# Base product of an expert-mixed FFN kernel by Strassen's algorithm over pairs of tiles

## What is computed

```python
y      = einsum('boi,bih->boh', agg_w, x) + agg_b[:, :, None]     # mixing over channels
base   = einsum('bsd,od->bso', y, base_W)                         # 1024 x 1024, the large product
logits = einsum('bsd,ed->bse', y, router_W)                       # 8 experts
rw     = top-2 of softmax(logits), divided by their sum
mid    = einsum('bsd,edr->bser', y, lora_A) * w_dense[..., None]  # 8 experts x rank 16 = 128 columns
out    = x + base + 2 * einsum('bser,erd->bsd', mid, lora_B)
```

## Time and profile before

| | |
|---|---|
| three runs | 1066.89, 1067.04, 1068.67 us; median 1067.04 |
| profiled execution | 1067.76 us, its span 1065.9 us |
| TensorE busy | 1050.6 us (99%) |
| VectorE busy | 444.5 us (42%) |
| ScalarE busy | 142.2 us (13%) |
| GpSimd busy | 18.9 us (2%) |
| mean granted TensorE clock | 0.995 |
| DMA | 79.64 MB, mean 75 GB/s |

### The profile page before, as it was taken

How to read it: one execution, slowest core, us unless ns; L and a number is a source line. 1 busy time by engine, 2 the same in 40 slices (tenths; PEclk the granted TensorE clock), 3 DMA queues, 4 the chain that set the end, 5 groups by cost and what they waited for, 6 DMA issues and landing times.

```text
span 1065.9 us, 17562 instructions
## 1 busy us (share of the span) xinstructions
PE 1050.6 (99%) x6386; PEld 1047.3 (98%) x6386; DVE 444.5 (42%) x1318; ACT 142.2 (13%) x310; POOL 18.9 (2%) x19
## 2 busy tenths in 40 slices
PE   6899999999999999999999999999999999999998
PEld 5899999999999999999999999999999999999998
DVE  5344344344344344344344344344344344344344
ACT  6311111111111111111111111111111111111110
POOL 4200000000000000000000000000000000000000
PEclk9899999999999999999999999999999999999999
DMA  7312212212212212212212212212212212212211
GB/s 208 112 44 87 83 48 86 78 51 86 82 47 86 75 54 86 74 56 86 72 57 86 73 56 86 71 58 86 67 62 86 66 63 86 68 61 86 69 39 60
DMA packets 48895, 79.64 MB, mean 75 GB/s; under 512 B 22472, under 2 KB 31432, under 8 KB 48848
## 3 DMA queue, kind: packets, MB, share of 16 engines
q1 hardware_dynamic: 39376, 45.87, 15.5%
q10 hardware_dynamic: 9504, 33.56, 8.0%
HBM read 43.76 MB, written 33.59 MB: 73 GB/s over the span
## 4 chain that ended last, share of the span: by engine, by line
PE 97%; DVE 1%; SPq 1%; DMA 0%; ACT 0%; issue 0%; DVEq 0%
PE acc L391 77%; PE y_ps L366 11%; PE acc L415 8%; PE acc L293 1%; PE y_ps L400 1%; DMA x_sb<-in_L_cond_weight 0%; DVE mixk L597 0%; PE y_ps L310 0%; DVE w_lo L572 0%; SPq L201 0%; DVE out_sb L696 0%; ACT mixk L487 0%; PE acc L345 0%; DVE agg L180 0%; SPq L194 0%
## 5 line engine op out<-in xcount | busy, mean ns | idle before, releaser
L391 PE MATMUL acc<-w_hi,y_hi 128*128 128x388 f32 (+1 forms) x1536 | 395.8, 364 | 0.6 <-DVE y_lo L638 0.6
L391 PE MATMUL acc<-w_hi,y_lo 128*128 128x388 f32 (+1 forms) x1536 | 356.7, 339 | 0.0
L391 PE MATMUL acc<-w_lo,y_hi 128*128 128x388 f32 (+1 forms) x1536 | 356.6, 338 | 0.0
L391 PEld LDWEIGHTS acc<-w_lo,y_hi 128*128 128x128 f32 x1536 | 277.7, 188 | 0.0
L391 PEld LDWEIGHTS acc<-w_hi,y_lo 128*128 128x128 f32 x1536 | 276.6, 188 | 0.0
L391 PEld LDWEIGHTS acc<-w_hi,y_hi 128*128 128x128 f32 x1536 | 247.9, 190 | 1.0 <-issue 0.9
L366 PE MATMUL y_ps<-mix_w,x_sb 128*128 128x128 f32 x1024 | 196.5, 275 | 0.0
L366 PEld LDWEIGHTS y_ps<-mix_w,x_sb 128*128 128x128 f32 x1024 | 186.4, 190 | 0.0
L643 DVE COPY logits<-acc 128x8 f32<-128x8 f32 x64 | 10.7, 167 | 296.0 <-PE acc L391 296.0
L630 DVE TENSOR_TENSOR y_sum<-y_ps,bias_sb 128x512 f32<-128x512 f32 x128 | 88.5, 691 | 78.6 <-PE y_ps L366 78.6
L638 DVE TENSOR_TENSOR y_lo<-y_sum,y_hi 128x512 fp32r<-128x512 f32 x128 | 88.0, 687 | 45.5 <-ACT y_hi L521 45.5
(11 more groups left out here) (76 smaller groups left out, 283.7 us busy)
## 6 DMA issues: line engine op xcount, KB each, us to landing
x_sb<-in_x SPq DMA_DIRECT2D x64, 512.0 KB, 4.8
out<-out_sb ACTq DMA_DIRECT2D x63, 512.0 KB, 4.9
w_stage<-in_L_ffn_base_W SPq DMA_DIRECT2D x8, 512.0 KB, 7.4
bias_sb<-bias_rows SPq DMA_DIRECT2D x64, 64.0 KB, 3.6
mix_w<-agg SPq DMA_DIRECT2D x126, 16.0 KB, 4.2
x_sb<-in_L_cond_weight SPq DMA_DIRECT2D x4, 128.0 KB
la_raw<-in_L_ffn_lora_A SPq DMA_DIRECT2D x8, 64.0 KB, 3.1
out_sb<-in_L_ffn_lora_B SPq DMA_DIRECT2D x1, 512.0 KB, 5.5
```

The lines of the kernel that those rows point to most:

```text
L391: last = nc.tensor.matmul(acc[s][g][:, 0:z - a], y[:, s, c * P:(c + 1) * P], w[:, c, a:z], start=(c == 0 and first), stop=(c == NC - 1 and ...
```

## The change

The base product is computed for two tiles at once, as a 2x2 by 2x2 block product in the seven-product form of Strassen's algorithm (Winograd's variant). The blocks are: rows by sample half, contraction by half (512), output by half (512).

- Operands of rows: A11, A12, A22 and the sums S1 to S4. VectorE writes the blocks (`add_bias`, four a pair), GpSimd makes the four sums (`sums`, `more_sums`), ScalarE the seven high parts (`split_high`), VectorE the seven low parts (`split_low`).
- Operands of weights: B11, B21, B22 and T1 to T4, made once in the setup, 28 groups where there were 16, three of the sums by GpSimd (2048 columns each) and T3 by accumulating products with `ident` and `neg_ident`.
- Products: seven of four chunks by three splits. Four of them carry a `lora_A` and router half at their end (`product_with_side`): each is two matmuls of 376 and 272 columns, the latter over two separate stretches of the weights and in a second PSUM bank. Three are single matmuls of 512 columns (`product`).
- The output halves are put together in `out_sb`, into which `x` has been loaded a second time: eight additions by VectorE (`add_into`), three of `u2` by GpSimd (`add_u2`), after one of VectorE that makes `u2`.
- `up` has 512 columns a matmul, four groups of three a pair, in the order P1, up21, up22, P2, P7, P6, P5, P4, up11, P3, up12, where the first two ups are of the pair before. The mixing products of the next pair stand behind the chunks of P1, P2, P7 and P6.
- The routing of the second tile of a pair is after P4, and P1 of the next pair waits for its end (`route_step`).
- `agg` goes out to DRAM (2 MB) and is read back as mixing weights in runs of 32 elements, with the channels of a sample in another order; x has two buffers; stores move from ScalarE's queue to SyncE's. All mixing of pair 0 stands in the setup.

The diff, cut to its core (the setup of the small network, tile names and removed lines are left out):

```diff
+    B11, B21, B22, T3, T1, T2, T4 = range(7)
+    BLOCK = HALF * BANK
+    SIDE0 = 7 * BLOCK
+    WCOLS = SIDE0 + NC * SD
+    LEAD = SD
+    HEAD = BANK - LEAD
+    A11, A12, S3, S2, S1, A22, S4 = range(7)
...
+            def load_x(n, m):
+                sp.wait_ge(y_ready, 4 * n + m - 1)
+                sp.dma_start(x_sb[m][:, :], x_t[2 * n + m, :, :]).then_inc(x_in[m], 16)
+                mixing_weights(2 * n + m, m)
...
+            def load_residual(p, k):
+                for s in range(2):
+                    if not (isinstance(p, int) and p < 2):
+                        sp.wait_ge(out_stored[k][s], 8 * (p - k))
+                    sp.dma_start(out_sb[k][s][:, :], x_rows[p, s, :, :]).then_inc(res_in[k][s], 16)
...
+            def body(p, k):
+                if not first(p):
+                    store(p - 1, 1 - k)
+                    if not last(p):
+                        load_residual(p + 1, 1 - k)
+                if not (isinstance(p, int) and p >= NP - 2):
+                    for m in range(2):
+                        load_x(p + 2, m)
...
+            def store(p, k):
+                sp.wait_ge(out11_up, p + 1)
+                sp.wait_ge(out12_done, p + 1)
+                sp.dma_start(out_rows[p, 0, :, :], out_sb[k][0][:, :]).then_inc(out_stored[k][0], 16)
+                sp.wait_ge(out21_up, p + 1)
+                sp.wait_ge(out22_up, p + 1)
+                sp.dma_start(out_rows[p, 1, :, :], out_sb[k][1][:, :]).then_inc(out_stored[k][1], 16)
...
+            pool.wait_ge(w_in[0], 16)
+            pool.wait_ge(w_in[2], 16)
+            nc.gpsimd.tensor_tensor(halves(t1_raw), w_raw[:, HIGH, D1], w_raw[:, LOW, D1],
+                                    ALU.subtract).then_inc(t_set, 1)
...
+            pool.wait_ge(w_tr, HALF * (T3 + 1))
+            pool.wait_ge(w_in[1], 16)
+            pool.wait_ge(t_set, 2)
+            nc.gpsimd.tensor_tensor(w_raw[:, HIGH, D1], w_raw[:, LOW, D2], halves(t2_raw),
+                                    ALU.subtract).then_inc(t_set, 1)
...
+            def sums(n):
+                pool.wait_ge(y_ready, 4 * n + 2)
+                nc.gpsimd.tensor_tensor(y_block(0, 1), y_block(0, 1), y_block(0, 0), ALU.subtract).then_inc(s3_set, 1)
+            def more_sums(n):
+                pool.wait_ge(y_ready, 4 * n + 4)
+                pool.wait_ge(s3_set, n + 1)
+                if not first(n):
+                    pool.wait_ge(op_lo_set[S2], n)
+                nc.gpsimd.tensor_tensor(s2[:, :], y_block(0, 1), y_block(1, 1), ALU.add).then_inc(s2_set, 1)
+                pool.wait_ge(s2_set, n + 1)
+                if not first(n):
+                    pool.wait_ge(op_lo_set[S1], n)
+                nc.gpsimd.tensor_tensor(s1[:, :], s2[:, :], y_block(0, 0), ALU.add).then_inc(s1_set, 1)
+                pool.wait_ge(op_lo_set[A12], n + 1)
+                nc.gpsimd.tensor_tensor(y_block(1, 0), y_block(1, 0), s2[:, :], ALU.subtract).then_inc(s4_set, 1)
...
+            def add_u2(p, k):
+                pool.wait_ge(u2_ready, p + 1)
+                pool.wait_ge(out22_p7, p + 1)
+                for s, half, done in ((1, 1, u2_in22), (0, 1, u2_in12), (1, 0, u2_in21)):
+                    pool.wait_ge(res_in[k][s], 8 * (p - k) + 16)
+                    o = out_sb[k][s][:, half * BANK:(half + 1) * BANK]
+                    nc.gpsimd.tensor_tensor(o, o, u2[:, :], ALU.add).then_inc(done, 1)
+            def body(p, k):
+                if not last(p):
+                    sums(p + 1)
+                add_u2(p, k)
+                if not last(p):
+                    more_sums(p + 1)
...
+            def product(o, blk, to, j, begin):
+                at = blk * BLOCK + j * BANK
+                for n, (y, w) in enumerate(SPLITS):
+                    mm = nc.tensor.matmul(to[:, 0:BANK], y[o][:, j * P:(j + 1) * P], w[:, at:at + BANK],
+                                          start=(begin and j == 0 and n == 0), stop=(j == HALF - 1 and n == 2),
+                                          skip_group_check=True)
+                return mm
+            def product_with_side(o, blk, to, j, half, begin):
+                at = blk * BLOCK + j * BANK
+                side = SIDE0 + (half * HALF + j) * SD
+                for n, (y, w) in enumerate(SPLITS):
+                    start, stop = (begin and j == 0 and n == 0), (j == HALF - 1 and n == 2)
+                    nc.tensor.matmul(to[:, LEAD:BANK], y[o][:, j * P:(j + 1) * P], w[:, at:at + HEAD],
+                                     start=start, stop=stop, skip_group_check=True)
+                    tail = bass.AP(w[:, :].tensor, at + HEAD, [[WCOLS, P], [side - at - HEAD, 2], [1, SD]])
+                    mm = nc.tensor.matmul(to[:, BANK:BANK + 2 * SD].rearrange("p (a n) -> p a n", a=2),
+                                          y[o][:, j * P:(j + 1) * P], tail, start=start, stop=stop,
+                                          skip_group_check=True)
+                return mm
...
+            def body(p, k):
+                mixing = not last(p)
+                wait_operand(A11, p)
+                if not first(p):
+                    pe.wait_ge(out11_p12, p)
+                    pe.wait_ge(route_step, 2 * ROUTE * p)
+                for j in range(HALF):
+                    mm = product_with_side(A11, B11, pa, j, 0, True)
+                    if j == HALF - 1:
+                        mm.then_inc(p1_mm, 1)
+                    if mixing:
+                        mix_chunk(p + 1, 0, j)
+                    if j == 1 and not first(p):
+                        pe.wait_ge(out11_up, p)
+                        transpose_mid(2 * p - 1)
+                if not first(p):
+                    wait_mid(2 * p - 1)
+                    up(0, pd, True, up21_mm)
+                    pe.wait_ge(out12_done, p)
+                    up(1, pc, True, up22_mm)
+                wait_operand(A12, p)
+                pe.wait_ge(p1_kept, p + 1)
+                for j in range(HALF):
+                    mm = product_with_side(A12, B21, pa, j, 1, False)
+                    if j == HALF - 1:
+                        mm.then_inc(p2_mm, 1)
+                    if mixing:
+                        mix_chunk(p + 1, 1, j)
+                wait_operand(S3, p)
+                if not first(p):
+                    pe.wait_ge(out21_p74, p)
+                    pe.wait_ge(side_b_kept, p)
+                for j in range(HALF):
+                    mm = product_with_side(S3, T3, pb, j, 0, True)
+                    if j == HALF - 1:
+                        mm.then_inc(p7_mm, 1)
+                    if mixing:
+                        mix_chunk(p + 1, 2, j)
+                wait_operand(S2, p)
+                if not first(p):
+                    pe.wait_ge(out21_up, p)
+                for j in range(HALF):
+                    mm = product(S2, T2, pd, j, True)
+                    if j == HALF - 1:
+                        mm.then_inc(p6_mm, 1)
+                    if mixing:
+                        mix_chunk(p + 1, 3, j)
+                wait_operand(S1, p)
+                if not first(p):
+                    pe.wait_ge(out22_up, p)
+                for j in range(HALF):
+                    mm = product(S1, T1, pc, j, True)
+                    if j == HALF - 1:
+                        mm.then_inc(p5_mm, 1)
+                    if j == 2:
+                        pe.wait_ge(u2_ready, p + 1)
+                        transpose_mid(2 * p)
+                wait_operand(A22, p)
+                pe.wait_ge(out22_p7, p + 1)
+                for j in range(HALF):
+                    mm = product_with_side(A22, T4, pb, j, 1, False)
+                mm.then_inc(p4_mm, 1)
+                if first(p):
                     pe.wait_ge(lb_lo_set, 1)
+                wait_mid(2 * p)
+                up(0, pd, True, up11_mm)
+                wait_operand(S4, p)
+                pe.wait_ge(out22_p5, p + 1)
+                for j in range(HALF):
+                    mm = product(S4, B22, pc, j, False)
+                mm.then_inc(p3_mm, 1)
+                up(1, pc, False, up12_mm)
+            over_pairs(pe, body)
+            pe.wait_ge(out11_up, NP)
+            transpose_mid(2 * NP - 1)
+            wait_mid(2 * NP - 1)
+            up(0, pd, True, up21_mm)
+            pe.wait_ge(out12_done, NP)
+            up(1, pc, True, up22_mm)
...
+            def keep_p1(p):
+                act.wait_ge(p1_mm, p + 1)
+                if not first(p):
+                    act.wait_ge(u2_ready, p)
+                    act.wait_ge(side_b_kept, p)
+                nc.scalar.activation(p1[:, :], pa[:, LEAD:LEAD + BANK + SD], ACT.Copy).then_inc(p1_kept, 1)
...
+                dve.wait_ge(p2_mm, p + 1)
+                route_logits(2 * p, pa[:, SLOG])
+                if mixing:
+                    add_bias(p + 1, 1)
+                route_choice(2 * p)
+                route_weigh(2 * p, pa[:, SMID])
+                if mixing:
+                    split_low(A11, p + 1)
```

(67 more changed lines are left out.)

823 lines of the change are left out of this document (422 added, 401 removed).

## The result

The changed kernel takes 1025.21 us (median of 4 runs, 1024.88 to 1027.29), against 1067.43 for the kernel before on the same chip: a ratio of 0.96, with a 95% interval of 0.9588 to 0.9613. The forecast was 1028.0. Its profiled execution took 1027.29 and has a span of 1025.6.

The account below looks back on a forecast made before the run. TensorE's work was taken as the bound: setup 55 plus 32 pairs of 29.2, corrected to 987.2, 31 stalls of 1.0 and a tail of 8.5 gave a span of 1026.7, so 1027.9 us; eight-in-ten range 992 to 1056.

Parts of the forecast that it names:

- A matmul's cost: On TensorE: 9.4 ns plus 0.4326 ns a column, so 230.9 ns for 512 columns, 172.1 for 376, 127.1 for 272.
- the pair's work: On TensorE in the loop: 29.20 us a pair against 32.03 before, 2.83 less, if nothing waits.
- Rival (c): TensorE's two-stretch matmul costs as one of 388 columns: +77 us, 1105 with the stall, 1074 without; chance 0.04.
- The stall: TensorE ahead of the next pair's P1, waiting for the second tile's routing: 1.0 us a pair, 31 us; 0.3 to 1.6 given 0.55.
- walk: Step through one pair's clock, with GpSimd and VectorE taking turns at SBUF: routing done at 30.1 plus 0.15, TensorE ready at 29.2.
- The setup: Everything ahead of the first pair's P1: ends at 55 us, bounds 49 and 62.
- The sum: Whole kernel: setup, 32 pairs, corrections, 31 stalls and a tail of 8.5 make a span of 1026.7 us.
- Outside the span: Addition from span to measured time, from the kernel before (1.9 over its span, 0.7 over its median): 1026.7 to 1027.9.
- (a): No stall, as GpSimd's sums are short enough or their turns fall elsewhere: 997 us; chance 0.22.
- (d): VectorE becomes the bound: 28.8 of 29.2 us a pair if every GpSimd sum excluded it; chance 0.10 together with Rival (b).
- Rival (b): Slower kernel: stall at SBUF turns passes 2.3 us a pair; 1109 with sums of 1.69; chance 0.10 together with (d).

Follow-up runs that it names:

- e1: Changed kernel, with GpSimd making s2, s1 and s4 of the next pair only after the second tile's routing has ended: 1001.54 us, ratio 0.9387.
- e2: Changed kernel, with P1 waiting only for the first tile's routing of the pair before, sums left in place: 1000.57 us, ratio 0.9368.
- e10: Changed kernel, with the second tile's logits added straight from PSUM in place of a copy between SBUF buffers: 1020.51 us, ratio 0.956.
- e8: Changed kernel, with lora_A and lora_B issued behind the first mixing weights and lora_A's GpSimd split behind T4: 1028.78 us, ratio 0.9633.
- e3: Changed kernel, with GpSimd making s2 twice, so that s1 and s4 come one sum later: 1077.51 us, ratio 1.0085.
- e6: Changed kernel with e2's relaxed wait and all derived weights ahead of the first pair's mixing, T4 before lora_A's split: 994.24 us, ratio 0.9304.

## Why the prediction was right

The mechanism was right on TensorE, and the total was right partly because two terms erred in opposite directions. Against the traces:

- **A matmul's cost, and the pair's work.** 29.20 was forecast and 29.13 measured (e1, e2). Rival (c), the form over two stretches at the price of 388 columns, did not occur.
- **The stall.** Its place, its cause and the wait that makes it cost were right, one a pair, 31 times. Its size was not: 1.0 forecast, 0.82 measured. The walk's error is in the turns, not in the price of a sum (1.25 taken, 1.28 to 1.30 measured undisturbed). It had `split_low(A12)` wait for the third `add_u2`; in the trace it began just ahead of it, at 535.90, took its 0.69, and the third `add_u2` took 1.81, so s2 started at 23.7 on the pair's clock, not 23.9. And it gave `beats` a turn between s1 and s4 and made `ties` wait for s4 until 27.9 on the pair's clock. In the trace s4 starts at once behind s1, and `beats` waits, until 27.7, with `ties` behind it. I had also not listed the copy of the logits, which has a single input, in SBUF; it was delayed as well (0.75), but e10 shows that its delay isn't what counted.
- **The setup.** "I take 55; bounds 49 and 62" is the step that failed: 64.0. It was mis-sized in the arrival of the mixing weights, put at 35 with the mixing done at 41; the mixing ran from 41.5 to 48. By the trace of the changed kernel, these 6.5 are four terms. "`agg` is whole at about 21" was 25.4: 4.4 late, and why was not tested. The way out and back was put at 14 and took 10.5 (6.8 out, 3.7 back), so -3.5. Between them lie 3.0 on SyncE's queue: the sum allowed for a queue full of weights, not for lora_A's eight issues, 17.97 us, which end at 34.4. And 2.6 pass between the weights' landing and the bias row's, which the same semaphore counts and the sum didn't name. Only the queue's term has a run: e8 takes that block away from the mixing's path and starts it at 37.3. With the setup's own spread of 2 us, all five profiles lie at or over the bound. T3 took 7.2 (47.9 to 55.1), not 4 to 5, another 2.1; T4's 4.57 was as forecast.
- **The sum.** P1(0) was 9.0 later than forecast. The first pair took 30.9 for 31.5 (94.91 - 63.99), each of the next thirty 29.94 for 30.2, by (993.24 - 94.91) / 30, so 7.7 less; from the last P1 to the span's end it took 32.4 for 34.2 (29.2 - 3.5 + 8.5), where the sum took 4.9 for a store, and the page has 2.9 for the median store of the changed kernel. 9.0 - 0.6 - 7.7 - 1.8 = -1.1, which is 1026.7 against a span of 1025.6. The stall's error alone is 0.18 x 31 = 5.6, the pair's own work 0.07 a pair, and the setup's error is +9.0.
- **Outside the span.** I added 1.2. The profiled execution lay 1.7 over its span, and 2.1 over the median, as it was the slowest of the four; the 1.2 came from an execution of the kernel before that lay 1.9 and 0.7 over.
- **Rivals (a) and (d).** VectorE did not become the bound: 67% busy. Nor was there no stall; where it is taken away, the time is 1001 (e1, e2), against the 997 of rival (a), and there the late setup shows without its counterweight.
- **Rival (b)** needed one more sum in the window: e3, at 1077.5, is slower than the kernel before. Its threshold was 2.3 a pair; e3's pairs are 31.53 - 29.13 = 2.40 over the pair without a stall, and the clock's part in that, 0.35, had no term in my walk. Its own way there, sums of 1.45 and more, did not come: they took 1.28 to 1.30, and the third `add_u2` was longer only by VectorE's turn.

What stays open: why the clock fell in seven of e3's pairs and not in the others, why `agg` was whole 4.4 later than forecast, and what the wait for the bias row costs in all. Executions of one kernel differ by 0.7 to 3.2 us. Each lies 1.7 to 1.8 over its own span, so a median can lie 3.5 over the profile's span (e8, where the fastest of the four was profiled) or 0.4 under it (e6, the slowest). Differences of that size between medians are read here only where the traces agree.

## What to carry to other kernels

Where an engine is freed of work, look for the semaphore that its next step waits for: here a wait for a whole routing, where half of it was needed, cost 24.6 of 1025 us, and one number removed it. In a setup, walk every queue with all it issues, since removing one late arrival pays only up to the next (11.7, 6.6, 7.1, then 2.1 us in this kernel), and look for buffers that share bytes and for semaphores that count more than their waiter reads (2.6 us ahead of the first mixing, 3.2 of e6's wait). A total that comes out right is no proof of its terms: compare each of them.
